# Row maxima of an attention kernel turned by VectorE's 32x32 transposes instead of TensorE's, with the shift pieces made on 128 partitions

## The reference

```python
q = proj(Wq) * scaling; k = proj(Wk); v = proj(Wv)
logits = einsum('abhqc,abhkc->abhqk', q, k) + nonbatched_bias[:, None]   # layer 1: + (mask - 1) * 1e9
weights = softmax(logits, axis=-1)
wavg = einsum('abhqk,abhkc->abhqc', weights, v)
gate = sigmoid(in_data @ Wg.T + gating_bias)
out = (gate * wavg) @ Wo.T + bo
x = x + out
```

## Time and profile before

| | |
|---|---|
| median of 3 runs | 3712.91 us (3711.34 to 3713.08) |
| profiled execution | 3713.87 us, its span 3712.1 us |
| TensorE busy | 3487.4 us, 94% of the span |
| VectorE busy | 3470.5 us, 93% |
| ScalarE busy | 2890.9 us, 78% |
| GpSimd busy | 3022.9 us, 81% |
| q1, the transfers that SyncE issues | 241680 packets, 251.85 MB, 38.3% of 16 engines |
| q10, those that ScalarE issues | 208896 packets, 201.38 MB, 19.6% |
| chain that ended last | PE 92%, DVE 3%, DMA 3%, issue 1% |

### The profile page before, as it was taken

One profiled execution on the slowest core, in us unless ns is written; L12 is line 12 of the kernel. 1 busy time (PEld: TensorE's weight loads), 2 busy tenths in 40 slices (PEclk: granted clock), 3 DMA queues, 4 the chain that ended last, 5 costly groups with the idle time before them and its releaser, 6 DMA issues.

```text
span 3712.1 us, 122419 instructions
## 1 busy us (share of the span) xinstructions
PE 3487.4 (94%) x36360; PEld 2625.9 (71%) x36360; DVE 3470.5 (93%) x11689; ACT 2890.9 (78%) x5393; POOL 3022.9 (81%) x2056
## 2 busy tenths in 40 slices
PE   0499999999999999999969999999999999999997
PEld 0377777777777777777747777777777777777775
DVE  6599999999999999999959999999999999999997
ACT  0388888888888888888857777778777777777785
POOL 1288888888888888888857888888888888888887
PEclk9999999999999999999989999999999999999999
DMA  8555555555555555555535556566556665566653
GB/s 319 176 117 117 116 115 117 114 119 116 116 115 116 117 117 116 115 118 114 117 112 112 118 117 118 116 121 119 117 117 119 117 121 117 117 118 117 119 119 76
DMA packets 450645, 454.09 MB, mean 122 GB/s; under 512 B 42880, under 2 KB 445440, under 8 KB 445968
## 3 DMA queue, kind: packets, MB, share of 16 engines
q1 hardware_dynamic: 241680, 251.85, 38.3%
q10 hardware_dynamic: 208896, 201.38, 19.6%
HBM read 182.39 MB, written 67.24 MB: 67 GB/s over the span
## 4 chain that ended last, share of the span: by engine, by line
PE 92%; DVE 3%; DMA 3%; issue 1%; POOL 1%; SPq 1%; ACT 1%; DVEq 0%; POOLq 0%; ACTq 0%
PE proj_b L743 19%; PE proj_a L743 18%; PE av_bank L770 13%; PE max_bank L754 13%; PE exp_bank L759 12%; PE proj_a L797 9%; PE den_bank L777 6%; PE proj_b L788 2%; DMA bias_k<-in_xT 1%; DVE stats L589 1%; DMA k_stack<-k_lo 1%; DVE max_bank L656 1%; DVE probs L669 0%; SPq L334 0%; POOL probs_sum L415 0%
## 5 line engine op out<-in xcount | busy, mean ns | idle before, releaser
L656 DVE CUSTOM_DVE_ANT_0 max_bank<-max_bank,bias_q 128x256 f32<-128x256 f32 x4096 | 1643.8, 443 | 156.4 <-PE max_bank L754 132.5
L415 POOL TENSOR_TENSOR probs_sum<-probs 128x1024 f32<-128x1024 f32 x512 | 1208.2, 2360 | 291.2 <-ACT probs L439 152.5
L669 DVE TENSOR_TENSOR probs<-exp_bank,bias_k 128x512 f32<-128x512 f32 x2048 | 1391.7, 680 | 7.4 <-PE exp_bank L759 7.4
L754 PE MATMUL max_bank<-k_stack,q_stack 96*128 96x256 f16 (+1 forms) x4096 | 788.0, 273 | 13.9 <-DMA k_stack<-k_lo 11.9
L759 PE MATMUL exp_bank<-q_stack,k_stack 100*128 100x256 f16 x4096 | 783.2, 272 | 9.6 <-DVE probs L669 6.3
L439 ACT ACTIVATE probs<-probs,mask_bias 128x1024 f32<-128x1024 f32 x512 | 572.8, 1148 | 61.4 <-DVE probs L669 61.2
L656 DVE DVE_READ_ACCUMULATOR2_ANT row_max<- 128x1 f32 x4096 | 573.1, 140 | 0.0
L442 ACT ACTIVATE probs<-probs 128x1024 f32<-128x1024 f32 x512 | 524.7, 1053 | 51.4 <-DVE probs L669 51.4
L770 PE MATMUL av_bank<-probs,v_sb 128*32 128x256 f32 x8192 | 549.3, 386 | 3.1 <-ACT probs L439 1.6
L754 PEld LDWEIGHTS max_bank<-k_stack,q_stack 96*128 96x128 f16 (+1 forms) x4096 | 381.2, 98 | 166.0 <-DVE row_max L656 104.3
L759 PEld LDWEIGHTS exp_bank<-q_stack,k_stack 100*128 100x128 f16 x4096 | 394.2, 97 | 72.6 <-DVE probs L669 11.5
(11 more groups left out here) (132 smaller groups left out, 7049.9 us busy)
## 6 DMA issues: line engine op xcount, KB each, us to landing
q_stack<-q_hi SPq DMA_DIRECT2D x512, 128.0 KB
k_stack<-k_hi SPq DMA_DIRECT2D x512, 128.0 KB
x_in<-in_xT ACTq DMA_DIRECT2D x128, 256.0 KB, 2.7
q_stack<-q_lo SPq DMA_DIRECT2D x256, 128.0 KB
k_stack<-k_lo SPq DMA_DIRECT2D x256, 128.0 KB
y<-in_xT ACTq DMA_DIRECT2D x128, 256.0 KB, 2.9
layer_out<-y ACTq DMA_DIRECT2D x128, 256.0 KB, 2.7
x_in<-layer_out ACTq DMA_DIRECT2D x128, 256.0 KB, 2.7
```

Of the source, the lines that this page charges most:

```text
L415: pool.tensor_tensor(probs_sum[:, g], pr[:, :, 0, :], pr[:, :, 1, :], ALU.add).then_inc(sum_ready, 1)
L656: op = dve.tensor_tensor_reduce(out=max_bank[h % 2][:, t, :], in0=max_bank[h % 2][:, t, :], in1=bias_q[:, h, t, :], scale=1.0 / FINE, scal ...
L669: dve.tensor_tensor(probs[:, r.ring(2), h], exp_bank[h % 2][:, :, :], bias_k[:, h], ALU.add).then_inc(logits_ready, 1)
L754: op = pe.matmul(bank_[:, t, :], q[0:n, t * P:(t + 1) * P], k[0:n, :], start=True, stop=True)
```

## The change

The way of the maxima into the stack is made anew.

- VectorE, step 0 of slot s: one transpose in blocks of 32x32 turns row s-2's `row_max`, read twice side by side, into `max_turned` (128 partitions x 32). A partition then holds one head and half for 32 queries, and the second 16 partitions of each group of 32 hold the same once more. After that step's logits it makes `coarse` (scaled, float16) and `max_kept` (times 0 or 1 per partition, from the new constant `piece_scale`).
- VectorE, step 1, between the two halves of the maximum: one instruction makes `pieces`, the coarse piece on one half of the partitions and the fine piece on the other, float16, 128 x 32.
- SyncE waits once, for `pieces`, and issues four transfers, each of 32 partitions x 64 bytes into rows 98 and 99 of the stack, then (second layer) the constants.
- TensorE's transposes, its waits for `fine_ready` and the constant `ident` go, as do ScalarE's `coarse` and VectorE's `fine`.
- VectorE's loop holds two slots instead of four; the place in `gate_tanh`, a ring of four, is then computed from the loop counter. VectorE no longer waits for `shift_psum`, for `av_psum` and `sum_ready` ahead of its logits (for `den_psum` instead), nor for `gate_ready`.

```diff
-def slots(engine, layer, body):
+def slots(engine, layer, body, unroll=UNROLL):
...
-    with engine.Fori(FIRST_LOOP // UNROLL, LAST_LOOP // UNROLL) as turns:
-        for u in range(UNROLL):
-            body(Row(layer, turns, u))
+    with engine.Fori(FIRST_LOOP // unroll, LAST_LOOP // unroll) as turns:
+        for u in range(unroll):
+            body(Row(layer, turns, u, unroll))
...
                 if r.active():
                     i, b = r.ring(4), r.ring(2)
-                    wait(sp, coarse_ready, r.count(1, 1), sp_passed)
+                    wait(sp, pieces_ready, r.count(1, 1), sp_passed)
+                    for p in range(P // HC):
+
+                        sp.dma_start(stack[0][MASK_ROW + 2:MASK_ROW + 4, i].rearrange(
+                            "w h (t p e) -> w (h t) p e", p=P // HC, e=HC)[:, :, p],
+                            pieces[HC * p:HC * (p + 1), b]).then_inc(shift_in[i], 16)
                     if l == 1:
                         sp.dma_start(stack[0][MASK_ROW:MASK_ROW + 2, i], a["k_rows"][0:2]).then_inc(shift_in[i], 16)
-                    sp.dma_start(stack[0][MASK_ROW + 2:MASK_ROW + 3, i], coarse[:, b]).then_inc(shift_in[i], 16)
-                    wait(sp, fine_ready, r.count(1, 1), sp_passed)
-                    sp.dma_start(stack[0][MASK_ROW + 3:MASK_ROW + 4, i], fine[:, b]).then_inc(shift_in[i], 16)
...
-                    act.wait_ge(shift_psum, r.count(1, 1))
...
-                    act.activation(coarse[:, i], shift_ps, ACT.Copy, scale=-FINE / COARSE).then_inc(coarse_ready, 1)
...
             def maxima(r, h):
+                of = r.plus(-1)
...
-                if h == 0:
-                    wait(dve, shift_psum, r.plus(-2).count(1, 1))
                 wait(dve, max_psum, r.count(8, h + 1), dve_passed)
                 for t in range(TT):
-
+                    if h == 1 and t == 1 and of.active():
+                        shift_pieces(of)
...
-                    wait(dve, av_psum, r.plus(-2).count(2, h // 4 + 1))
-                    wait(dve, sum_ready, r.plus(-2).count(2, h // 4 + 1))
+                    wait(dve, den_psum, r.plus(-2).count(2, h // 4 + 1))
...
-            def fine_shift(r):
-                i = r.ring(2)
+            def turn_maxima(r):
+                dve.wait_ge(max_done, r.count(8, 8))
+                dve.transpose(max_turned[:, :].rearrange("p (w j) -> p w j", w=2),
+                              row_max[:, r.ring(2)].unsqueeze(1).broadcast_to([P, 2, HEADS * TT])).then_inc(max_turn, 1)
+
+            def coarse_pieces(r):
+                dve.wait_ge(max_turn, r.count(1, 1))
+                dve.tensor_scalar(coarse[:, :], max_turned[:, :], -FINE / COARSE, None, ALU.mult)
+                dve.tensor_scalar(max_kept[:, :], max_turned[:, :], piece_scale[:, 1:2], None, ALU.mult
+                                  ).then_inc(coarse_ready, 1)
+
+            def shift_pieces(r):
                 dve.wait_ge(coarse_ready, r.count(1, 1))
-                dve.scalar_tensor_tensor(out=fine[:, i], in0=coarse[:, i], scalar=COARSE / FINE, in1=shift_ps,
-                                         op0=ALU.mult, op1=ALU.add).then_inc(fine_ready, 1)
+                dve.scalar_tensor_tensor(out=pieces[:, r.ring(2)], in0=coarse[:, :], scalar=piece_scale[:, 0:1],
+                                         in1=max_kept[:, :], op0=ALU.mult, op1=ALU.add).then_inc(pieces_ready, 1)
...
-                slots(dve, l, slot)
+                slots(dve, l, slot, 2)
...
-            def maxima_rows(r):
-                pe.wait_ge(max_done, r.count(8, 8))
-                if r.plus(1).active():
-                    pe.wait_ge(gate_ready, r.plus(1).count(1, 1))
-                wait(pe, fine_ready, r.plus(-1).count(1, 1))
-                i = r.ring(2)
-                for t in range(TT):
-                    op = pe.transpose(shift_ps[:, t * P:(t + 1) * P], row_max[:, i, t], ident[:, :])
-                op.then_inc(shift_psum, 1)
...
                         wait(pe, gate_ready, s.plus(-1).count(1, 1))
-                        wait(pe, fine_ready, s.plus(-2).count(1, 1))
                         project(s, 1, pb, 0, None)
```

More of the change, by code:

```diff
@@ L63, with __init__ @@
 class Row:
-    def __init__(self, layer, turns, off):
-        self.layer, self.turns, self.off = layer, turns, off
+    def __init__(self, layer, turns, off, unroll=UNROLL):
+        self.layer, self.turns, self.off, self.unroll = layer, turns, off, unroll
     def plus(self, n):
-        return Row(self.layer, self.turns, self.off + n)
+        return Row(self.layer, self.turns, self.off + n, self.unroll)
     def active(self):
@@ L143, in build @@
         group_avg = sb("group_avg", [P, P], f32)
-        ident = sb("ident", [P, P], f32)
         ones = sb("ones", [P, HC], f32)
@@ L174, in build @@
         gate_tanh = sb("gate_tanh", [P, 4, HG, TOK], f32)
-        row_max = sb("row_max", [P, 2, TT, HEADS], f32)
-        coarse = sb("coarse", [HEADS, 2, TOK], f16)
-        fine = sb("fine", [HEADS, 2, TOK], f16)
+        row_max = sb("row_max", [P, 2, HEADS * TT], f32)
+        piece_scale = sb("piece_scale", [P, 2], f32)
+        max_turned = sb("max_turned", [P, 2 * HEADS * TT], f32)
+        max_kept = sb("max_kept", [P, 2 * HEADS * TT], f32)
+        coarse = sb("coarse", [P, 2 * HEADS * TT], f16)
+        pieces = sb("pieces", [P, 2, 2 * HEADS * TT], f16)
         probs = sb("probs", [P, 2, HEADS, TT, TOK], f32)
@@ L228, in build @@
         max_psum, max_done = sem("max_psum"), sem("max_done")
-        coarse_ready, fine_ready = sem("coarse_ready"), sem("fine_ready")
-        shift_psum = sem("shift_psum")
+        max_turn, coarse_ready, pieces_ready = sem("max_turn"), sem("coarse_ready"), sem("pieces_ready")
         shift_in = [sem(f"shift_in{i}") for i in range(4)]
-        SHIFT_INC = [2 * 16, 3 * 16]
+        SHIFT_INC = [4 * 16, 5 * 16]
         exp_psum, logits_ready = sem("exp_psum"), sem("logits_ready")
@@ L266, in _ @@
             sp.dma_start(group_avg[:, :], a["group_avg"]).then_inc(const_in, 16)
-            sp.dma_start(ident[:, :], a["ident"]).then_inc(const_in, 16)
+            sp.dma_start(piece_scale[:, :], a["piece_scale"]).then_inc(const_in, 16)
             for i, n in enumerate(("L0_conv_gating_bias", "L1_conv_gating_bias")):
@@ L704, in slot @@
                         maxima(s.plus(-1), step)
+                    if step == 0 and s.plus(-2).active():
+                        turn_maxima(s.plus(-2))
                     if step == 3 and s.plus(-4).active():
@@ L710, in slot @@
                         logits(r, h)
-                    if step == 1 and s.plus(-2).active():
-                        fine_shift(s.plus(-2))
+                    if step == 0 and s.plus(-2).active():
+                        coarse_pieces(s.plus(-2))
+                    if step == 0 and s.plus(-2).active() and not s.plus(-1).active():
+                        shift_pieces(s.plus(-2))
                     r = s.plus(-4)
@@ L803, in slot @@
                 for step in range(8):
-                    r = s.plus(-2)
-                    if step == 1 and r.active():
-                        maxima_rows(r)
                     r = s.plus(-1)
@@ L888 @@
     mask_rows[0], mask_rows[1] = COARSE, FINE
+    piece_scale = np.zeros((P // HC, 2, HC // 2, 2), np.float32)
+    piece_scale[:, 0, :, 0], piece_scale[:, 1, :, 0], piece_scale[:, 1, :, 1] = 1.0, COARSE / FINE, 1.0
+    piece_scale = piece_scale.reshape(P, 2)
     arrays = {
@@ L898 @@
         "group_avg": np.kron(np.eye(P // GROUP, dtype=np.float32), np.full((GROUP, GROUP), 1.0 / GROUP, np.float32)),
-        "ident": np.eye(P, dtype=np.float32),
+        "piece_scale": piece_scale,
         "k_rows": stack_rows,
```

22 lines of the change are left out of this document (10 added, 12 removed).

## The result

The changed kernel takes 4082.55 us in the median (4079.92 to 4149.49); the kernel before took 3712.61 us beside it. The 4149.49 is one execution of four, 1.6% above the others, and the ratio leaves it out: it is 1.099, with a 95% interval of 1.0975 to 1.1006. The prediction said 3619 us, with a range to 3770: the sign was wrong and the time lies outside the range.

What follows compares the result with a forecast made beforehand. TensorE set the pace at 13.61 us per slot, VectorE 0.6 behind. New slots of 13.19 (VectorE, first layer) and 13.30 (transfer loop, second) gain 54 and 40, together 94 us: 3619 us, range 3590 to 3770.

Steps and rivals of the forecast that it cites:

- the hole in front of the K projection: TensorE's idle place after the exp_bank pair, attributed to waiting for `fine_ready`; its removal was to save 0.25 us per slot.
- the hole stays: Rival: TensorE's idle place before the K projection remains as "issue"; slot 13.39, 3657 us, chance 0.08.
- TensorE's own 13.14: TensorE's forecast slot in us: 13.61 less 0.22 for the transposes and 0.25 for the wait before the K projection.
- 13.19: VectorE's forecast slot in us: 12.55 plus 0.64 for four small instructions, between 12.95 and 13.47; bound of the first layer.
- Their waits should cost nothing: VectorE's four new instructions: their waits would be covered by other work; if not, each adds some 0.1 us.
- The transfer loop: SyncE's issues, then the 7.73 us stack stream to TensorE's first maximum: slot 11.14 + 4c, second layer 11.41 + 4c.
- c: Issue time on SyncE of each of the four new pieces transfers: taken as 0.47 us, bounds 0.24 and 0.75.
- break-even at 0.58: Issue time per new SyncE transfer, in us, at which both layers' loops average the old slot of 13.61.
- 1.46 + 4c: Time in us from TensorE's second maximum to SyncE's issue of the first q_hi, after the four pieces issues.
- 3605 us: Total if SyncE's issue time went with the engine count, near k_rows, leaving the slot at VectorE's bound in both layers.
- It holds, with 0.4 to spare: Pieces land before the next row's first exp: there at 4.6 us (second layer 5.1), wanted at 5.49.
- queue rival: SyncE's four issues ahead of q_hi become the bound: 3833 us at c = 0.70, 3750 at 0.62; chance 0.26.

Runs made afterwards that it cites:

- both causes away: Changed kernel with turned and kept maxima in PSUM and only one of the four pieces transfers: 3602.19 us, ratio 0.970.
- twins: Changed kernel, one transfer, turned maxima in PSUM, pieces instruction moved into GpSimd's key sum; kept maxima in PSUM: 3765.92 us, in SBUF: 4553.49 us.
- late twin: Changed kernel, one transfer, pieces instruction moved into GpSimd's key sum, turned maxima in PSUM but kept maxima in SBUF: 4553.49 us.

## Why the prediction was wrong, point by point

**TensorE.** Right. The transposes are gone, and so is the hole in front of the K projection: 1006.53 to 1006.75 is 0.22, where the earlier trace rows had 0.49. The rival "the hole stays" is out. With both causes away the kernel reached 13.16, so TensorE's own 13.14 was not too low by more than 0.02.

**VectorE's own work.** The price of the four instructions was near. In the kernel with both causes away the four instructions cost, to the next start, 0.13, 0.10, 0.16 and 0.16, together 0.55 where 0.64 was taken. VectorE's slot is then 12.55 + 0.55 = 13.10 by the prediction's own sum, under TensorE's 13.14, and not 13.19; that 13.19 lies so near the measured 13.16 is in part luck, since TensorE sets that slot. The step that failed stands beside it: "Their waits should cost nothing". I looked only for waits on semaphores. I bounded an instruction without a row by a cheap one (the reciprocal, 0.23 at most) and did not ask which operands it has or what runs on GpSimd at that moment. The old `fine` had one operand in PSUM, as `avg` has, so no row of the old slot could show the effect. The new one reads two from SBUF and takes 1.7 to 2.35 us beside a key sum; this was worth 263 of the 370 us, and the range didn't hold it.

The Trainium skill states this. "SBUF — State Buffer", section "Who interferes with whom", says that a VectorE instruction with two SBUF inputs contends with a GpSimd instruction that reads SBUF, and that one with at most one SBUF input outside the 2-port modes does not. The twins agree with it: 1.90 us with two SBUF inputs, 0.23 with one. The same section lets an instruction with one SBUF input contend if it runs in a 2-port mode ("Whoever issues first gets the shared pair for the whole instruction"), which agrees with `coarse`: 0.76 us from SBUF, 0.18 from PSUM. No run shows that `coarse` runs in such a mode. The rule of the Trainium skill was there to be weighed and would have given a rival of its own; I did not weigh it.

**The transfer loop.** The mechanism was right, the size of one term wrong. The rival gave 14.21 in the second layer at c = 0.70 and the slot is 14.25. The term that was mis-sized is c: taken 0.47 as the middle between the rows of 0.24 and 0.70, measured 0.67 in the loop and 0.65 alone. Above the break-even at 0.58 the sign turns. The choice of the middle had no ground: of the rows that I had, all from SBUF (0.60 to 0.70) were long, and those with two partitions at the far end were also those from DRAM with long rows, so their 0.24 could not be put down to the two partitions. One more small term: `k_rows` behind the pieces takes 0.43, not 0.24. With c = 0.67 and this the second layer's loop is 11.41 + 2.68 + 0.19 = 14.28, against 14.25. (The parts of 1.46 + 4c as the prediction lists them add up to 1.43; the gap in front of `q_hi` that it gives as 0.16 is 0.19 in the earlier trace rows, and with this the 1.46 is right.)

For c I had weighed a rule of the Trainium skill ("DMA: Bandwidth & Descriptors", section "Why a DMA increments its semaphore by 16 and not by 1"), on which number of engines a transfer is spread, and had asked whether the issue time goes with that number; this would have given 3605 us. The issue of two partitions from SBUF to two takes 0.60 us, so the trace disagrees with that use of it.

**The first layer, put together.** 11.14 + 4 x 0.67 = 13.82 from the loop. The pieces end 2.61 us after the second maximum (1004.54 to 1007.15) and not 1.09: 1.52 more. The stream takes 8.02 from the first `q_hi` to the first maximum and not 7.73: 0.29 more. Together 15.63, against 15.56 in this slot and 15.68 in the mean. The 0.29 was not traced to a cause.

**The pieces' landing.** "It holds, with 0.4 to spare" failed where the pieces came late: first exp waits for them 0.92 us (1011.11). In the kernel with four transfers and PSUM operands, TensorE's waits in the first layer have no such row, so this too came from the collision.

**The chances.** The mean slot of two causes could not come out of rivals that each held one. The queue rival alone, at its measured size, is 3820 us, which also lies outside my range to 3770: I had cut it where c = 0.62, though the rows from SBUF on that queue were at 0.60 to 0.70, all but one of them above 0.62.

## What to carry to other kernels

Before a new VectorE instruction is priced, list where each of its operands lies and what GpSimd runs beside it: an operand in PSUM may be worth more than the instruction costs. A price between two groups of rows is not their middle; find what each group has in common with the new one, and if the sign hangs on it, take the group that differs in fewer respects. Where a queue's issues stand in front of a stream that the next row waits for, their number times their issue time is the change, however few bytes they carry.

## What the runs showed of the hardware that I had not expected

A 32-column VectorE instruction with two SBUF operands takes 0.24 us alone and 1.7 to 2.35 us beside GpSimd's 2.35 us addition; it ends 0.04 to 0.05 us behind it. A `tensor_scalar` from float32 in SBUF to float16 in SBUF waits in the same way (0.76 us beside GpSimd's subtraction, 0.17 alone). The stall is counted as busy time of VectorE: the changed kernel's 91% holds it. The two can meet in every slot of a stretch (32 of 32 slots from 1000 to 1500 us) and not meet in the other layer of the same program.

In the late twin TensorE's granted clock was 0.50 (1.2 GHz, the lower of its two levels) for some 3 us behind a wait of 2.14 us (1002.04 to 1005.00), and 1.00 from 1005.40 on; its mean of 0.90 over 192 to 1880 us is what some 3.4 us at 0.50 in each slot of 17.06 give. Behind the waits of 0.92 and 1.13 us in the changed kernel it stayed at 1.00. So the late instruction cost 1.67 us of each slot in waiting and 1.59 more in slow products.

An issue on SyncE takes 0.56 to 0.67 us for 2 to 4 KB from SBUF, from two partitions to two as from eight to one, but 0.24 for two whole 4 KB rows from DRAM when nothing is right in front of it, and 0.43 behind four issues of the pieces.
